# The layout of the gated values: slots of a patch side by side instead of patches of a slot side by side

## The reference, cut to what matters

```python
h = einsum('oc,bchw->bohw', w_in, gn(x))            # 32 -> 170 channels
h = irfft2(rfft2(patches(h)) * fft_filter)          # 8 x 8 patches, 144 in an image
y = conv(h, dw_k)                                   # 3 x 3, each channel by itself
g = gelu(y[:, :85]) * y[:, 85:]                     # the gate
x = x + einsum('oc,bchw->bohw', w_out, g)           # 85 -> 32 channels
```

## Time and profile before

| what | value |
|---|---|
| median of 3 runs | 3460.51 us (3444.41 to 3466.08) |
| profiled execution, span | 3457.4 us |
| TensorE matmuls (PE), busy | 2908.9 us, 84% |
| TensorE weight loads (PEld), busy | 2020.6 us, 58% |
| VectorE (DVE), busy | 1847.5 us, 53% |
| ScalarE (ACT), busy | 1311.5 us, 38% |
| GpSimd (POOL), busy | 253.1 us, 7% |
| second part, first image's transposes to the last | 1251.2 to 3451.1 us |

### The profile page before, as it was taken

One profiled execution on the slowest core, in us unless ns is written; L12 is line 12 of the kernel. 1 busy time (PEld: TensorE's weight loads), 2 busy tenths in 40 slices (PEclk: granted clock), 3 DMA queues, 4 the chain that ended last, 5 costly groups with the idle time before them and its releaser, 6 DMA issues.

```text
span 3457.4 us, 164388 instructions
## 1 busy us (share of the span) xinstructions
PE 2908.9 (84%) x74374; PEld 2020.6 (58%) x74374; DVE 1847.5 (53%) x4198; ACT 1311.5 (38%) x2217; POOL 253.1 (7%) x274
## 2 busy tenths in 40 slices
PE   4699999999996788888888888888888888888887
PEld 4355554555453666666666666666656666666665
DVE  3356565565652245554556555655555555555555
ACT  1234444444342233343434343433433333443332
POOL 2011111111110200000000000000000000000000
PEclk9899999999998599999999999999998999999999
DMA  6578778787764334334443444334433444334433
GB/s 126 124 170 172 164 169 170 172 171 165 165 144 69 32 100 111 95 93 104 117 106 89 107 119 105 89 99 105 116 97 89 105 115 112 89 99 113 113 92 84
DMA packets 451958, 404.16 MB, mean 117 GB/s; under 512 B 404172, under 2 KB 404478, under 8 KB 447497
## 3 DMA queue, kind: packets, MB, share of 16 engines
q1 hardware_dynamic: 446030, 376.93, 47.5%
q10 hardware_dynamic: 5228, 16.70, 1.4%
HBM read 165.77 MB, written 78.16 MB: 71 GB/s over the span
## 4 chain that ended last, share of the span: by engine, by line
PE 49%; DVE 6%; issue 5%; ACT 3%; DMA 3%; ACTq 2%; SPq 1%; POOL 0%; DVEq 0%; POOLq 0%
PE ps L1295 12%; PE ps L1245 10%; PE ps L1280 10%; PE ps L1309 9%; PE ps L1263 8%; DMA neighbours<-border 3%; DVE gated L1356 3%; ACT gelu L1180 2%; DVE channels_first L1369 2%; ACTq L1190 2%; ACT hidden_patches L1153 1%; DVE border L1163 1%; SPq L1052 1%; ACT border L1163 0%; DMA x_normed<-in_L_conv_w_in_dram 0%
## 5 line engine op out<-in xcount | busy, mean ns | idle before, releaser
L1356 DVE TENSOR_TENSOR gated<-gelu,ps 128x432 f32<-128x432 f32 (+1 forms) x512 | 289.3, 567 | 555.8 <-ACT gelu L1180 529.7
L449 ACT ACTIVATE hidden<-ps,hidden_scale 128x576 f32<-128x576 f32 x512 | 351.7, 738 | 614.5 <-PE ps L554 614.5
L1369 DVE STREAM_TRANSPOSE channels_first<-gated 128x512 f32<-128x512 f32 x576 | 571.3, 1043 | 1.1
L1153 ACT COPY hidden_patches<-ps 128x704 f32<-128x704 f32 x576 | 406.5, 749 | 434.3 <-PE ps L1245 434.2
L1280 PE MATMUL ps<-hidden_patches,channel_tables 64*64 64x144 f32 x11264 | 403.4, 287 | 97.4 <-DVE gated L1356 97.4
L1263 PE MATMUL ps<-hidden_patches,channel_tables 64*64 64x144 f32 x11264 | 405.7, 287 | 90.2 <-DVE border L1163 84.8
L568 PE MATMUL ps<-hidden,taps 128*32 128x288 f32 x6144 | 437.3, 417 | 43.1 <-DMA taps<-conv_tables 29.7
L1245 PE MATMUL ps<-w_in_t,x_normed 32*64 32x88 f32 x18432 | 422.3, 259 | 54.2 <-issue 49.3
L1263 PEld LDWEIGHTS ps<-hidden_patches,channel_tables 64*64 64x64 f32 x11264 | 359.4, 134 | 184.6 <-ACT border L1163 114.7
L1163 ACT COPY border<-ps 128x432 f32<-128x432 f32 (+1 forms) x512 | 226.4, 495 | 618.9 <-DVE border L1163 216.9
L554 PE MATMUL ps<-x_rows,taps 32*64 32x288 f32 x12288 | 455.0, 415 | 2.5 <-issue 1.3
(11 more groups left out here) (147 smaller groups left out, 1328.7 us busy)
## 6 DMA issues: line engine op xcount, KB each, us to landing
neighbours<-border SPq DMA_DIRECT2D x1024, 126.8 KB
taps<-conv_tables SPq DMA_DIRECT2D x192, 216.0 KB
x_image<-in_x_dram SPq DMA_DIRECT2D x128, 288.0 KB, 5.8
x<-x_image SPq DMA_DIRECT2D x128, 288.0 KB, 4.7
x_image<-x SPq DMA_DIRECT2D x384, 96.0 KB
out_dram<-x_image SPq DMA_DIRECT2D x384, 96.0 KB, 2.0
x_rows<-in_x_dram SPq DMA_DIRECT2D x512, 60.0 KB
neighbours<-border ACTq DMA_DIRECT2D x1024, 15.8 KB
```

The lines of the kernel that those rows point to most:

```text
L449: A(hid[T % 3][:, 2 * h:2 * h + 2, :, 1:1 + W], ps1[:, 2 * h:2 * h + 2, 0:XB * W].rearrange("p c (k w) -> p c k w", k=XB), ACT.Relu, scale ...
L1153: nc.scalar.copy(o, i).then_inc(s_we[pair], 1)
L1356: TT(o, gl[odd][:, 0:n * NPC].rearrange("p (t m) -> p t m", m=NPC), ps[:, 2 * odd + 1, 0:n * NPC].rearrange("p (t m) -> p t m", m=NPC), AL ...
L1369: last = nc.vector.transpose(t[:, s], g)
```

## The change

The tile `gated` changes its layout from slot by patch to patch by slot. The gate writes the same elements with a step of 44 words between one patch and the next; the transpose reads runs of 32 neighbouring words, one run for each patch. Element counts, types, the order of the instructions and the waits stay as they are. The table of the set-up, which takes the tile as one run, is not affected.

```diff
-        gt = sb("gated", [P, NT4, NPC])
+        gt = sb("gated", [P, NPC, NT4])
...
-                o = gt.rearrange("p (t s) n -> p t s n", s=2)[:, CUT[s]:CUT[s + 1], odd, :]
+                o = gt.rearrange("p n (t s) -> p t s n", s=2)[:, CUT[s]:CUT[s + 1], odd, :]
                 TT(o, gl[odd][:, 0:n * NPC].rearrange("p (t m) -> p t m", m=NPC),
                    ps[:, 2 * odd + 1, 0:n * NPC].rearrange("p (t m) -> p t m", m=NPC), ALU.mult).then_inc(s_m, 1)
...
                     first = s * (NT4 - SB)
-                    g = gt[:, first:first + SB, :].rearrange("p t (q i) -> p q i t", q=NQUAD)[:, :, WSTEP * v:WSTEP * v + WSTEP, :]
+                    g = gt[:, :, first:first + SB].rearrange("p (q i) t -> p q i t", q=NQUAD)[:, :, WSTEP * v:WSTEP * v + WSTEP, :]
                     last = nc.vector.transpose(t[:, s], g)
```

## The result

The changed kernel takes 3517.99 us (median of 4 runs, 3514.32 to 3536.36) beside 3457.55 us for the kernel before in its four runs: a ratio of 1.021, 95% interval 1.0164 to 1.0256, about 60 us slower. Run again in a later call (`e0_after_again`) the ratio was 1.0158, interval 1.0122 to 1.0193. The time lies inside the stated range (3440 to 3605), but outside the forecast's own (3470 to 3502) and above its 3483 us; of the cases it is rival 2 that came nearest (3528).

What follows compares the result with a forecast made beforehand. The gates' end was taken to set a closed TensorE loop in the set stage, most transposes being hidden. Gates +95, transposes -27, clock -45 us gave +23 us, about 3483 us (+0.7%); own range 3470 to 3502, stated range 3440 to 3605.

Steps and rivals of the forecast that it cites:

- rival 2: Clock falls do not go, because a 1.68 us gap in the seventh set is enough: +68 us, 3528 us; chance 0.16.
- The transposes: VectorE transposes reading runs of 32 neighbouring words: 1043 to 687 ns each, 27 us saved of 205 us busy time.
- the head's wait: TensorE's wait for the first transposes of an image's step stage: 0.70 us shorter, 22 us over 32 images.
- the gap at the head: TensorE's gap before the first `w_out` of an image: from 1.90 to 1.46 us.
- the last image: Steps with no `w_in` to fill TensorE: 8 steps x 0.66, 5 us saved.
- The gates: VectorE gates writing one word in 44, in the set stage's loop: 903 and 655 ns, costing 95 us in 32 images.
- The period of the full sets: Time from one `hidden` to the next in the set stage: 5.15 us, against 4.78 before.
- the seventh set's gap: TensorE's gap before `hidden` of the seventh set: grows from 1.31 to 1.68 us.
- The clock: TensorE's clock falls behind long gaps, worth 48 us: 45 us taken as saved with the head's gap shortened.
- granted clock of 1.00 in most images: Sign to be seen in the profile after; wrong if intervals below 1.00 are as many as before, 23 of 31.
- The dearest row: Upper bound for the gates, from a strided write 128 words apart at 2.13 ns a column: 1078 and 771 ns.
- the middle of the nearest rows: Gate price taken between writes 32 and 54 words apart (885 and 921 ns for 432 columns): 903 and 655 ns.

Runs made afterwards that it cites:

- e0_after_again: The changed kernel run again, unchanged, in a later call against the kernel before: ratio 1.0158, interval 1.0122 to 1.0193.
- the second pair of traces: Kernel before and changed kernel each run again, unchanged, in a later call for traces: kernel before 3451.58 us in its one run, changed kernel at ratio 1.0158.
- the kernel before filled: Kernel before plus four extra matmuls, results unread, in TensorE's gap at each head of the step stage: 3413.33 us beside 3435.12, ratio 0.9932.
- the write alone: Kernel before with only the strided gate writes, transposes still reading one word in 144, output wrong: 3554.33 us beside 3435.12, ratio 1.0336.

## Why the prediction was right or wrong, step by step

**The transposes, right.** 687 ns forecast, 685 measured; the head's wait 0.69 us shorter, 0.70 forecast (transpose to `w_out` 2.05, then 1.36 us in the timelines); the gap at the head 1.46 forecast, 1.47 measured; the last image 5.5 us shorter. Of 202 us of busy time saved, the rest was hidden, as forecast.

**The gates, right in mechanism, a little small.** 903 and 655 ns forecast, 955 and 685 measured. What limited the damage to the sum is that a longer pair overlaps more: 1.76 us for two of 0.955, so 0.15 us and not 0.09. The period of the full sets is 5.18 us (5.15 forecast), the seventh set's gap 1.68 us, exactly the forecast. The images without a fall in it have a set stage of 39.53 us in place of 36.51, 3.02 us (2.97 forecast). That this comes so near is in part luck: the dearer gate and the larger overlap were both missed, and they cancel. The set stage's 103 us are 31 x 3.02 = 94 and some 9 more, and these are the clock: the four images where it falls in this stage take 41.97 us there, 4 x 2.4 = 10 us more than the others.

**The clock, the step that failed.** "I take 45 of the 48 us as saved" was the term that was mis-sized: by the intervals the falls went from 47 to 40 us, a saving of 7, and in the second pair of traces from 22 to 30 us, none. In the first pair the falls of the step stage came to some 17 us less, and those of the set stage, which had none before, to some 10. The direct terms carry the result: the two traces differ by 55 us, which are 64 in the images without a fall and 3 ahead of them, less 7 in the falls and 5.5 in the last image. The size of 48 us was itself read from one trace; the second trace of the kernel before and the kernel before filled give 22.

The gaps came out as forecast. What was wrong is to take gaps between 1.33 us, behind which the clock had held, and 1.90 us, behind which it fell, for harmless "since each stands alone between long runs of matmuls". Counted by place over the 14 traces, the falls behind the 31 heads go with the head's gap: none at 0.38 to 1.21 us (six kernels), 3 at 1.40 us (48 words), 10 at 1.44 us (46 words), 10, 12 and 15 at 1.47 us, 20 and 22 at 1.90 us, 27 at 2.14 us (the write alone). Those in the set stage go with its longest gap: none in the kernels where it is 1.27 to 1.58 us, one to four where it is 1.62 to 1.68 us. From one to nine falls a trace lie elsewhere, most of them late in the step stage, and what they follow is open.

So rival 2 described the result, at a chance of 0.16: its price (68 us) was near, its place only in part. Of the 19 falls in the kernel after 4 lie in the set stage and 10 behind the head, whose gap of 1.47 us I had taken for harmless. That the time still fell into the stated range is the width of that range; the sign "granted clock of 1.00 in most images" did not come (14 of 31), and more of the chance lay within 1% (0.46) than on slower (0.42).

**The bounds.** The dearest row (2.13 ns a column) was too dear, the middle of the nearest rows too cheap: 44 words cost 1.88 ns. The Trainium skill, "Vector Engine (DVE) Microarchitecture Reference", section 5.2, has 2.50 ns for a destination stepping 24 words and 1.71 ns for a hop of 4 KiB, and says that small steps cost more than large ones. The runs agree with it from 44 words on: 44, 46 and 48 words, at 1.88, 1.79 and 1.77 ns, lie between and fall with the step. The 32 words of the earlier trace rows, at 1.69 ns (a copy of one size), do not fit it.

**What stays open.** Why 44 words are dearer than 32. What a fall costs: the same cut gives 2.1 us for an image with one in the first trace of the kernel before, and 0.95 us in the second. What the falls late in the step stage follow. Whether the number of the seventh set's falls depends on those of the head.

## What to carry to other kernels

When an access has to be strided on one side, put the stride on the instruction that nobody waits for: 202 us of VectorE's time were saved where TensorE was busy anyway, 125 us were spent inside a closed loop between two engines, and the loop won. Read from the timeline, for each instruction that gets longer or shorter, who starts when it ends; the busy column doesn't say. And count a change of the clock as saved only if the gap in front of it goes away: a gap shortened from 1.90 to 1.47 us still had a fall behind 10 to 15 of 31 heads, one of 1.21 us or less behind none. Another order of TensorE's work, which closed the gap with useful matmuls, gave 71 us, some 16 of them by the clock.

## What the hardware showed that was not expected

- The price of a single-word write depends on its step in a way that padding can use: four unused words a patch took the gate from 955 to 901 ns, two took it to 923 (one run each).
- Matmuls whose result nobody reads made the kernel before 0.7% faster: they shorten no wait, and what changed with them is the granted clock (30 of 31 intervals at 1.00).
- Two overlapping strided gates hide 0.15 us of each other, two plain ones 0.09 us.
